# Keys' maximum over the partitions in the first layer of a four-layer kernel: TensorE transposition and product with ones in place of GpSimd's collective

## The reference

```
def softmax_kernel(x, proj, is_query):
    norm = x.shape[-1] ** (-0.25)
    ratio = proj.shape[0] ** (-0.5)
    xp = jnp.einsum('bhnd,md->bhnm', x * norm, proj)
    diag = jnp.sum(jnp.square(x), axis=-1, keepdims=True) * 0.5 * (norm * norm)
    if is_query:
        stab = jnp.max(xp, axis=-1, keepdims=True)
    else:
        stab = jnp.max(xp, axis=(-1, -2), keepdims=True)
    return ratio * (jnp.exp(xp - diag - stab) + EPS_K)
...
qp = softmax_kernel(q, proj, is_query=True)
kp = softmax_kernel(k, proj, is_query=False)
k_sum = jnp.sum(kp, axis=2)
denom = jnp.einsum('bhnm,bhm->bhn', qp, k_sum)
ctx = jnp.einsum('bhnm,bhnd->bhmd', kp, v)
out = jnp.einsum('bhnm,bhmd->bhnd', qp, ctx) / denom[..., None]
attn = out.transpose(0, 2, 1, 3).reshape(b, n, d) @ Wo.T + bo
x = layer_norm(video + attn, g2, be2)
```

## Time and profile before

| | us |
|---|---|
| median of 3 runs | 1899.73 (1899.47 to 1908.59) |
| the profiled execution, its own time | 1918.26 |
| its span in the profile | 1916.5 |
| of it, first layer (to the last write of `X` there) | 385.2 |
| round 0, rounds 1 and 2, rounds 3 to 6, round 7 | 46.2; 34.5 and 33.7; 38.7 to 40.1; 34.2 |

### The profile page before, as it was taken

One profiled execution on the slowest core, in us unless ns is written; L12 is line 12 of the kernel. 1 busy time (PEld: TensorE's weight loads), 2 busy tenths in 40 slices (PEclk: granted clock), 3 DMA queues, 4 the chain that ended last, 5 costly groups with the idle time before them and its releaser, 6 DMA issues. The chain is left out here.

```text
span 1916.5 us, 26699 instructions
## 1 busy us (share of the span) xinstructions
PE 1544.6 (81%) x8728; PEld 972.5 (51%) x8733; DVE 1281.5 (67%) x3212; ACT 1026.1 (54%) x1747; POOL 792.2 (41%) x909
## 2 busy tenths in 40 slices
PE   4587777549999999867639999999997587899990
PEld 1344434326666666533215555555553566677770
DVE  1456666456777778547858877877883564688874
ACT  2254445313666665624524667776766444577762
POOL 1124342443455554414661122221100366488876
PEclk8789999756999999979957999999999588899995
DMA  7600000031222221000045444434430011344424
GB/s 215 219 1 1 1 1 1 1 115 37 93 72 76 75 72 40 16 12 1 1 91 125 119 124 126 114 92 118 120 89 2 23 59 45 124 134 128 136 63 132
DMA packets 96201, 144.30 MB, mean 75 GB/s; under 512 B 31266, under 2 KB 59939, under 8 KB 91952
## 3 DMA queue, kind: packets, MB, share of 16 engines
q1 hardware_dynamic: 91072, 134.11, 25.1%
q0 software_dynamic: 4992, 8.48, 1.3%
HBM read 104.19 MB, written 57.48 MB: 84 GB/s over the span
## 5 line engine op out<-in xcount | busy, mean ns | idle before, releaser
L1165 DVE TENSOR_REDUCE ctx_nm<-ctx_s 128x1 f32<-128x512 f32 x512 | 329.4, 680 | 96.9 <-PE ctx_s L1441 96.1
L1277 ACT ACTIVATE ctx_probs<-ctx_st 128x1024 f32<-128x1024 f32 x256 | 254.2, 1022 | 114.8 <-PE ctx_st L1457 110.6
L1165 DVE TENSOR_REDUCE rope_nm<-rope_s 128x1 f32<-128x128 f32 (+3 forms) x512 | 230.1, 480 | 89.6 <-PE rope_s L1444 87.2
L1277 ACT ACTIVATE rope_probs<-rope_st 128x1024 f32<-128x1024 f32 (+1 forms) x256 | 172.3, 702 | 142.3 <-PE rope_st L1457 141.3
L1441 PE MATMUL ctx_s<-ctx_kst,ctx_qst 96*128 96x512 f32 x512 | 221.0, 469 | 17.6 <-DMA ctx_kst<-ctx_contexts 8.6
L1441 PE MATMUL rope_s<-rope_kst,rope_qst 96*128 96x128 f32 (+3 forms) x512 | 185.7, 395 | 4.4 <-DVE rope_nm L1165 3.2
L1030 POOL TENSOR_SCALAR_AFFINE_SELECT rope_probs<-rope_probs 128x256 f32<-128x256 f32 x256 | 98.3, 409 | 173.8 <-ACT rope_probs L1277 173.4
L1441 PEld LDWEIGHTS ctx_s<-ctx_kst,ctx_qst 96*128 96x128 f32 x512 | 100.5, 197 | 131.3 <-DVE ctx_nm L1165 53.6
L1457 PE MATMUL ctx_st<-ctx_qst,ctx_kst 98*128 98x512 f32 x512 | 164.9, 405 | 2.3 <-ACT ctx_probs L1277 2.3
L1457 PE MATMUL rope_st<-rope_qst,rope_kst 98*128 98x512 f32 (+3 forms) x512 | 141.9, 361 | 3.9 <-ACT rope_probs L1277 3.9
L2631 DVE TENSOR_TENSOR sw_hf<-sw_silu,sw_u 128x512 f32<-128x512 f32 x124 | 84.5, 682 | 83.0 <-ACT sw_silu L2401 57.2
(11 more groups left out here) (376 smaller groups left out, 3341.8 us busy)
## 6 DMA issues: line engine op xcount, KB each, us to landing
sw_raw<-in_L_ffn_all SPq DMA_DIRECT2D x24, 768.0 KB
sw_xs<-in_pad SPq DMA_DIRECT2D x65, 260.0 KB, 9.9
rope_halves<-rope_qk SPq DMA_DIRECT2D x24, 512.0 KB
ctx_halves<-ctx_qk SPq DMA_DIRECT2D x24, 512.0 KB, 6.2
ctx_qst<-ctx_contexts SPq DMA_DIRECT2D x32, 384.0 KB
ctx_kst<-ctx_contexts SPq DMA_DIRECT2D x32, 384.0 KB
rope_qst<-rope_halves SPq DMA_DIRECT2D x32, 192.0 KB
rope_kst<-rope_halves SPq DMA_DIRECT2D x32, 192.0 KB
```

What stands on the lines that cost most here:

```text
L1165: nc.vector.tensor_reduce(nm[:, g, j * T + t:j * T + t + 1], bank("s", b, n)[:, 0:keys], AXX, ALU.max, negate=True).then_inc(s_used, 1)
L1277: nc.scalar.activation(probs[n // GH % 2][:, n % GH, u * units[0]:u * units[0] + units[u]], st_bank[u][:, 0:units[u]], ACT.Exp, scale=SCAL ...
```

## The change

The maximum over the partitions is taken in four steps in place of one: PE transposes `km` into a bank (16 partitions x 128), DVE reduces that to one number for each head (`row`), DVE multiplies the identity with it (`diag`, 16 x 16), and PE multiplies a matrix of ones with `diag`, so that each of 128 partitions gets all 16 maxima in a bank. `shift_keys` reads this bank. Both banks are of the `dve` ring, between `wo` and `qx`. The orders of PE, DVE and ACT are rearranged around it: the query product of `project` goes ahead of the transposition, the key product between the two new PE steps, the value products behind query features 1, `widen` ahead of query features 2 and 3. On DVE `shift_keys` goes ahead of `offsets(2, g)` and `shift_queries(m, 0)`. On ACT the keys' exponents go first, the queries' first exponents behind the ReLUs. The last `residual` of a batch moves behind `divide` of the next round, which makes one more round. `unit` is a new 16x128 tile of ones, filled once.

```
-        IN_ROUND = {"dve": [("wo", 1, 1), ("qx", 0, T)],
+        IN_ROUND = {"dve": [("wo", 1, 1), ("km", 0, 1), ("stab", 0, 1), ("qx", 0, T)],
...
+            def turn_maxima(m):
+                dst = claim("km", m)
+                pe.wait_ge(km_ready, m + 1)
+                nc.tensor.transpose(dst[0:H, 0:P], km[:], ident[:]).then_inc(kmT_ps, 1)
+
+            def spread_maxima(m):
+                dst = claim("stab", m)
+                pe.wait_ge(spread_ready, m + 1)
...
+                nc.tensor.matmul(dst[:, 0:H], unit[:], diag[:], start=True, stop=True).then_inc(stab_ps, 1)
...  (order of PE in a round)
+                if within(f):
+                    project(f, "q")
                 if within(m):
+                    turn_maxima(m)
+                if within(f):
+                    project(f, "k")
+                if within(m):
+                    spread_maxima(m)
                     query_features(m, 0)
                     query_features(m, 1)
                 if within(f):
-                    project(f)
+                    project_values(f)
+                if within(e):
+                    widen(e)
                 if within(m):
                     query_features(m, 2)
                     query_features(m, 3)
-                if within(e):
-                    widen(e)
...  (POOL)
-            def largest_key(m):
-                pool.wait_ge(km_ready, m + 1)
-                nc.gpsimd.partition_all_reduce(stab[:], km[:], P, RMAX).then_inc(stab_ready, 1)
...
-                if within(m):
-                    largest_key(m)
...  (DVE)
+            def largest_of_batch(m):
+                dve.wait_ge(kmT_ps, m + 1)
+                nc.vector.tensor_reduce(row[:], bank("km", m)[0:H, 0:P], AXX, ALU.max).then_inc(row_ready, 1)
+                dve.wait_ge(row_ready, m + 1)
+                if m:
+                    dve.wait_ge(stab_ps, m)
+                nc.vector.tensor_scalar(diag[:], ident[0:H, 0:H], row[:], None, ALU.mult).then_inc(spread_ready, 1)
...  (order of DVE in a round)
+                if within(b - 4):
+                    residual(b - 4)
+                if within(m):
+                    largest_keys(m)
                 if within(g):
                     spread(2, r2)
                 if within(m):
-                    largest_keys(m)
+                    largest_of_batch(m)
                 if within(g):
                     moments(2, g)
                 if within(a):
                     with_input(a)
                 if within(m):
-                    shift_queries(m, 0)
+                    shift_keys(m)
                 if within(g):
                     offsets(2, g)
                 if within(m):
-                    shift_keys(m)
+                    shift_queries(m, 0)
...
                 if within(g):
                     moments(3, g)
                     offsets(3, g)
-                    residual(g)
...  (order of ACT in a round)
                 if within(m):
-                    query_exponents(m, 0)
+                    key_exponents(m)
                 if within(g):
                     normalise(2, g, x2, r2, n2_ready)
-                if within(m):
-                    key_exponents(m)
                 if within(e):
                     rectify(e)
                 if within(m):
+                    query_exponents(m, 0)
                     query_exponents(m, 1)
...
                 if within(g):
+                    if g:
+                        act.wait_ge(done, g)
                     normalise(3, g, x3, x2, n3_ready)
```

More of the change, by code:

```diff
@@ L153, in performer_layer @@
         feats, hsel, bmask = sb("feats", [P, H * M]), sb("hsel", [P, 32]), sb("bmask", [P, P])
-        ones, floor, eps, half = sb("ones", [P, 32]), sb("floor", [P, P]), sb("eps", [P, 1]), sb("half", [P, T])
+        ones, unit, floor, eps, half = sb("ones", [P, 32]), sb("unit", [H, P]), sb("floor", [P, P]), sb("eps", [P, 1]), sb("half", [P, T])
         stats = [sb(f"stats{k}", [P, T, 6]) for k in range(4)]
@@ L161, in performer_layer @@
         dgT, dg = sb("dgT", [64, S]), ring("dg", 2, [P, T, 64])
-        kmx, km, stab, ck = sb("kmx", [P, T, H]), sb("km", [P, H]), sb("stab", [P, H]), sb("ck", [P, T, H])
+        kmx, km, row, diag, ck = sb("kmx", [P, T, H]), sb("km", [P, H]), sb("row", [H, 1]), sb("diag", [H, H]), sb("ck", [P, T, H])
         qmx, cq = sb("qmx", [P, T, H]), sb("cq", [P, T, H])
@@ L190, in performer_layer @@
         within = lambda b: 0 <= b < B
-        rounds = range(-2, B + 3)
+        rounds = range(-2, B + 4)
         both = lambda t: slice(2 * t, 2 * t + 2)
-        IN_ROUND = {"dve": [("wo", 1, 1), ("qx", 0, T)],
+        IN_ROUND = {"dve": [("wo", 1, 1), ("km", 0, 1), ("stab", 0, 1), ("qx", 0, T)],
                     "act": [("x1T", 2, 1), ("yT", -1, 1), ("q", -1, 1), ("k", -1, 1), ("v", -1, 1), ("dg", -1, 1), ("dgt", -1, 1),
@@ L208, in emptied @@
         def emptied(name, c, k):
-            return {"wo": (r_ready, c + 1), "x1T": (x1T_ready, c + 1), "qx": (qx_used, c * T + k + 1), "yT": (yT_ready, c + 1),
+            return {"wo": (r_ready, c + 1), "km": (row_ready, c + 1), "stab": (ck_ready, c + 1), "x1T": (x1T_ready, c + 1), "qx": (qx_used, c * T + k + 1), "yT": (yT_ready, c + 1),
                     "q": (qk_ready, 2 * c + 1), "k": (qk_ready, 2 * c + 2), "v": (v_ready, c + 1), "dg": (dgT_ready, c + 1),
@@ L263, in key_features @@
                 nc.tensor.matmul(held[t][:], tile(kT[m % 2], t), feats[:], start=True, stop=True).then_inc(kx_ps, 1)
+            def turn_maxima(m):
[5 more added lines that the diff above has]
+                pe.wait_ge(spread_ready, m + 1)
+                if m == 0:
+                    pe.wait_ge(constants_ready, 1)
+                nc.tensor.matmul(dst[:, 0:H], unit[:], diag[:], start=True, stop=True).then_inc(stab_ps, 1)
             def query_features(m, t):
@@ L272, in turn_input, with project @@
                 transposed(dst, lambda t: y[:, t, :], yT_ps)
-            def project(f):
+            def project(f, name):
                 if f == 0:
@@ L277, in project, with project_values @@
                 pe.wait_ge(yT_ready, f + 1)
-                nc.tensor.matmul(claim("q", f)[:], wq[:], yT[:], start=True, stop=True).then_inc(qk_ps, 1)
-                nc.tensor.matmul(claim("k", f)[:], wk[:], yT[:], start=True, stop=True).then_inc(qk_ps, 1)
+                nc.tensor.matmul(claim(name, f)[:], (wq if name == "q" else wk)[:], yT[:], start=True, stop=True).then_inc(qk_ps, 1)
+            def project_values(f):
                 dst = claim("v", f)
@@ L454, in _ @@
             ch.do(nc.gpsimd.memset(ones[:], 1.0))
+            ch.do(nc.gpsimd.memset(unit[:], 1.0))
             ch.do(nc.gpsimd.memset(floor[:], EPS_K))
@@ L517, in largest_keys @@
                 if m:
-                    dve.wait_ge(stab_ready, m)
+                    dve.wait_ge(kmT_ps, m)
                 nc.vector.tensor_reduce(km[:], kmx[:].rearrange("p t h -> p h t"), AXX, ALU.max).then_inc(km_ready, 1)
+            def largest_of_batch(m):
[5 more added lines that the diff above has]
+                nc.vector.tensor_scalar(diag[:], ident[0:H, 0:H], row[:], None, ALU.mult).then_inc(spread_ready, 1)
             def shift_keys(m):
-                dve.wait_ge(stab_ready, m + 1)
+                dve.wait_ge(stab_ps, m + 1)
                 dve.wait_ge(dg_ready, m + 1)
-                ch.do(nc.vector.tensor_tensor(ck[:], dg[m % 2][:, :, 32:32 + H], bc(stab[:], T), ALU.add))
-                ch.sync()
+                nc.vector.tensor_tensor(ck[:], dg[m % 2][:, :, 32:32 + H], bc(bank("stab", m)[:, 0:H], T), ALU.add).then_inc(ck_ready, 1)
+                dve.wait_ge(ck_ready, m + 1)
                 for t in range(T):
```

3 lines of the change are left out of this document (2 added, 1 removed).

## The result

The changed kernel takes 1882.2 us (median of 4, 1877.8 to 1884.4), the kernel before 1902.3 beside it: a ratio of 0.9896 with a 95% interval of 0.9873 to 0.9919, about 20 us or 1% faster. The forecast was 1870.0 in a range of 1861 to 1884; the gain it named was 29.7 us, so two thirds of it came.

What follows compares the result with a forecast made beforehand. A chain across engines, with POOL's silent 7.4 us behind the collective, was taken to bound each round. 15.5 - 2.0 + 11.6 + 4.2 + 0.4 = 29.7 us off the median 1899.7 gave 1870.0, range 1861 to 1884.

Steps and rivals of the forecast that it cites:

- the rival by which they would stay: POOL's 7.4 us idle belongs to its next instruction, not the collective; gain 0 to 4 us, 1898; chance 3%.
- The chain through ACT: ACT's queue from `v` to `dgT` bounds that stretch of round 4; `dgT` at 209.3, 4.5 us earlier than before.
- the sum's own band: Whole kernel: the forecast as summed, a gain of 24 to 34 us, 1866 to 1876; chance 62%.
- dear hops: Each of two PE-DVE hops costs 1.2 us and `diag` meets POOL, or slow value products; gain 17 to 22, about 1880; 17%.
- Rounds 3 to 6: `dgT` 4.5 us earlier less 1.6 for the clock: 2.9 us gained in each round, 11.6 together.
- The charge for the clock: PE's wait of 3.8 us ahead of `turn_lengths` leaves contexts partly at 1.2 GHz; 1.6 us lost per round, rounds 3 to 6.
- Round 0: `kp` starts at 41.8 and `dgT` comes at 51.1 in place of 66.68, a gain of 15.5 us.
- Rounds 1 and 2: DVE sets them and the collective was hidden; two hops, `row` and `diag` less saved waiting lose 1.0 us in each.
- Round 7: No lengths, so no gap ahead of contexts; by the same sum as the earlier rounds, a gain of about 4.2 us.
- Moving the residual: Worth nothing in rounds 3 to 7, hidden by `attend`; +0.4 us (0 to 1.4) in rounds 8 to 10.
- the one without a clock loss: PE stays at 2.4 GHz through contexts; rounds 3 to 6 gain 4.5 us each, 36 in all, 1864; chance 15%.
- a TensorE that stays slow: PE stays at 1.2 GHz from contexts through `narrow` and `attend`; 23.4 us slower, 1923; chance 3%.

Runs made afterwards that it cites:

- filled gap: Changed kernel with three unused 128x512 fp32 products on PE in the wait ahead of `turn_lengths`, from the second batch on; ratio 0.9830 to the kernel before.
- Order only: Changed kernel with POOL's collective back at the head of its round, the four new steps out, all new orders kept; ratio 1.0040 to the kernel before.
- residual only: Kernel before with the last `residual` moved behind the next round's `divide`, one more round and ACT's wait for `done`; ratio 1.0025.
- early load: Kernel before with one more collective on POOL ahead of the loop, its result unused; ratio 1.0016.
- late pads: Kernel before with SP's stores of zero pads for the last layer held back from round 0 to round 4; ratio 0.9989.
- two collectives: Kernel before with a second, unused collective straight ahead of each one; ratio 1.0004.
- contexts and queries first: Changed kernel with `contexts` ahead of `turn_lengths` on PE and `keep_queries` ahead of `input_norm` on ACT; ratio 0.9740 to the kernel before.
- no collective: Kernel before with POOL's collective replaced by a copy of `km` into `stab`, maximum over partitions left out, orders untouched; ratio 0.9782.

## Why the prediction was right, and where it was off

**The mechanism held, the size did not.** POOL's silent 7.4 us left with the collective; the rival by which they would stay is out. In round 4 `kp` came at +10.5 us from `divide` (forecast 10.7), `dgT` at +22.1 (21.7), the gap on PE was 3.77 us (3.8). The chain through ACT was the right one to follow. But the sum's own band was a gain of 24 to 34 us, and the times show 20 (15 to 24). 1882.2 lies inside the range because the range reached down to a gain of 17 for dear hops, and the hops were not dear. That the total fell inside is in part luck: other terms were too large by about as much as that rival would have cost.

**Rounds 3 to 6: 11.6 forecast, 8.4 in the first profiles, 9.2 by the means of two each.** The charge for the clock was too small: 1.6 us a round by the partial drop of the earlier trace rows. Round 3 cost just that (4.84 - 3.19 = 1.65), but in rounds 4 to 6 all of contexts ran at 0.51, and 5.82 - 3.19 = 2.63 us went. That is the term that failed, and filled gap gives it back. The row behind it did not repeat in before either: its second profile has a gap of 0.89 us in round 2 and 3.19 behind it. Order only has the partial drop at gaps of 2.1 to 2.4 us, so the price was right for a gap of that size and too low for 3.8. A further 0.4 went at `dgT`. ACT started on `v` 0.4 us later than forecast (at +13.05 from `divide`, not +12.7), and its last exponents waited 0.86 us for DVE, where `cq` had met `affine2` on POOL (0.95 us against 0.19); the prediction held that case to be just in time. ACT's own work was 0.7 shorter than summed and made up for most of that wait. Against these losses before's rounds 3 and 5 were longer than the round 4 that stood for all (40.1 and 39.8 against 39.1).

**Round 0: 15.5 forecast, 13.7 measured (12.1 by the means).** `dgT` came at 54.40, not 51.1. Not all of these 3.3 us show in the 13.7, since from `dgT` to `divide` it took 11.2 us in this profile and 12.6 in before's; in the second profile of the changed kernel it is 12.6 as well. These are rows of round 0 after:

```profile
40.31 0.26 DVE L535 TENSOR_REDUCE pf_km<-pf_kmx 128x16 f32<-128x64 f32 x1
...
41.25 1.08 DVE L543 TENSOR_SCALAR pf_diag<-ident,pf_row 16x16 f32<-16x16 f32 x1
41.27 1.04 POOL L443 TENSOR_TENSOR pf_sqq<-pf_qT 128x512 f32<-128x512 f32 x1 [4.97 <-ACT pf_qT L683]
...
47.75 3.37 PE L280 MATMUL pf_dve<-pf_feats,pf_qT 128*128 128x512 f32 x4 [2.17 <-DVE pf_qp L567]
...
53.44 1.06 ACT L709 ACTIVATE pf_qp<-pf_qp 128x1024 f32<-128x1024 f32 x1 [4.05 <-DVE pf_qp L567]
```

`km` itself was 0.9 us later; `diag` met `squares` and took 1.08 us, where the sum took 0.15 because POOL has nothing to do at that point in round 4; and PE, after a wait of 2.17 us, ran the last query features in 3.37 us instead of the 1.88 of before, with DVE waiting 1.16 and 1.02 us for them.

**Rounds 1 and 2: 1.0 lost each forecast.** The first profiles have 0.5 and 0.1 won. By the means of two profiles each (33.96 and 32.81 before, 34.81 and 33.67 after) they lose 0.85 each. Before's round 2 alone differs by 1.85 us between its two profiles, and the longer one, 33.73, is the exception: residual only, early load, late pads and two collectives, which change little or nothing there, have 31.6 to 32.2. A row of one execution is no base for a microsecond there.

**Round 7: 4.2 forecast, 1.7 measured.** The round has no projections, PE stands 1.97 us ahead of the product with ones, and the first four instructions of query features take 3.68 us together at 293.84, against 1.98 at 179.93 in round 4. "By the same sum" carried over the work of PE that this round doesn't have.

**The rest.** Moving the residual was worth nothing, as said; the tail gained 0.9, 0.4 forecast. In all the layer gained 25.4 us in the first profiles and 22.2 by the means, against 29.7. The times say 15 to 24 us in the first comparison and 9 to 20 in the second. Both hold 15 to 20, a little under the layer's 22.2; the difference is not settled, and the rest of the program varies by more than that from profile to profile. Of the rivals, the one without a clock loss (36 us) did not come by itself: filled gap (38.5 us off before's layer) and contexts and queries first (52.7) had to build it. Dear hops didn't come (0.35 and 0.49 us from PE's start to DVE's in round 4, not 1.2), nor did a TensorE that stays slow: it is back at 1.00 behind contexts.

## What to carry to other kernels

When a short instruction is followed by idle time that nothing explains, price the pair, and ask whether it is paid per call, per change of kind or once; and try what happens to its size beside DMA traffic. When a chain gets shorter on one engine, list the gaps that this opens on PE, and put ready work into them by order, following the next engine's queue as well, or the gap and the low clock only move on. Repeat the profile of before first: here two profiles of it were 3 us apart on the layer, more than several of the terms, and one price was read from a row that the second did not have.

## What the runs showed of the hardware

- POOL's `partition_all_reduce` is recorded with 0.39 us, but the change to it takes 5.6 to 6.3 us of POOL and the change back 6.7 to 7.9 us in quiet rounds; beside stores at 303 to 330 GB/s it was 9.3 to 14.7 and 10.4 to 13.6 us. A second call directly behind the first started 0.31 us later, with no gap of its own.
- The maximum of 128x16 over the partitions by transposition, reduction, diagonal and product with ones takes 0.27, 0.26, 0.22 and 0.39 us in round 4 of the changed kernel, and 3.1 us from the start of `km` to that of `ck` with other DVE work in between.
- A gap of 3.77 us on PE was followed by 5.8 us at 0.51 in rounds 4 to 6 of the changed kernel; in round 3 full clock still stood behind the same gap, and the mean over the next 5.1 us was 0.67. A gap of 2.83 us was followed by full clock in three rounds of no collective and by half clock in one. Unused products in the gap kept the clock at 1.00.
- Small DVE operations on SBUF stretched from about 0.2 us to about 1.0 where a POOL operation was running: `cq` 0.95, `diag` 1.08. `diag` has one tensor input and one number per partition, and was held as well. `ck` took 1.14 us with `stab` in SBUF (at 205.08 in before) and 0.22 with the maxima in a PSUM bank, both times with POOL at work when it started.
